# Delta rule layer: softplus, value convolution and key product moved to other slots of the iteration

## The reference

```
q, k, v = silu(causal_conv4(x @ W) + b)              per head
g    = -exp(A_log) * softplus(x @ Wfa @ Wfb + dt_bias)
beta = sigmoid(x @ Wb);  q = l2norm(q) * K**-0.5;  k = l2norm(k)
for each step t:
    S  = S * exp(g)
    vd = (v - S^T k) * beta
    S  = S + k vd^T;  o = S^T q
out = (o * rsqrt(mean(o*o) + eps) * o_norm * sigmoid(gate)) @ Wo
```

## Time and profile before

| | |
|---|---|
| median of 3 runs | 6179.44 us (6178.84 to 6185.34) |
| the profiled execution | 6183.02 us, its span 6181.4 us |
| mean granted clock of PE | 0.925 |
| busy share of the span | PE 80%, PEld 53%, DVE 63%, ACT 44%, POOL 34% |
| the delta rule's 64 iterations | from 1759.6 us on; the last one's Abs (L1875) at 4762.6 us |

### The profile page before, as it was taken

One profiled execution on the slowest core, in us unless ns is written; L12 is line 12 of the kernel. 1 busy time (PEld: TensorE's weight loads), 2 busy tenths in 40 slices (PEclk: granted clock), 3 DMA queues, 4 the chain that ended last, 5 costly groups with the idle time before them and its releaser, 6 DMA issues. The chain is left out here.

```text
span 6181.4 us, 82487 instructions
## 1 busy us (share of the span) xinstructions
PE 4972.5 (80%) x24879; PEld 3272.6 (53%) x24965; DVE 3916.5 (63%) x6588; ACT 2733.2 (44%) x4960; POOL 2091.4 (34%) x2663
## 2 busy tenths in 40 slices
PE   5788747999577888888888888888888665888856
PEld 3566534555245666666666666666666432444423
DVE  4677663222347777777777777777777344888756
ACT  5555351111124444544444444544454212777732
POOL 2455400110234544445444454454544144000100
PEclk8899878999779999999999999999999887999989
DMA  2011005344321111111111111111111034111110
GB/s 59 28 28 29 21 21 193 102 141 154 124 64 55 37 42 37 48 54 44 42 41 48 50 46 40 47 42 41 45 46 30 13 129 136 55 54 53 44 56 27
DMA packets 355561, 365.98 MB, mean 59 GB/s; under 512 B 100192, under 2 KB 253280, under 8 KB 353920
## 3 DMA queue, kind: packets, MB, share of 16 engines
q1 hardware_dynamic: 335472, 286.73, 15.7%
q0 software_dynamic: 19744, 74.99, 3.5%
HBM read 264.76 MB, written 96.86 MB: 59 GB/s over the span
## 5 line engine op out<-in xcount | busy, mean ns | idle before, releaser
L1811 POOL TENSOR_TENSOR delta_rule_suffix<-delta_rule_suffix,delta_rule_prefix 128x256 f32<-128x256 f32 x448 | 499.0, 1114 | 1192.4 <-ACT delta_rule_prefix L1905 767.6
L2152 PE MATMUL delta_rule_proj<-delta_rule_hT,delta_rule_w_qkv 128*128 128x512 f32 x1024 | 468.1, 600 | 0.0
L2176 PE MATMUL delta_rule_level<-delta_rule_qk_second,delta_rule_k_first 128*128 128x128 f32 x3072 | 426.0, 283 | 51.5 <-DVE delta_rule_L_small L1984 40.1
L2176 PEld LDWEIGHTS delta_rule_level<-delta_rule_qk_second,delta_rule_k_first 128*128 128x128 f32 x3072 | 386.1, 195 | 100.0 <-issue 77.9
L481 DVE TENSOR_TENSOR_SCAN scan_hs<-scan_decay,scan_inp 128x512 f32<-128x512 f32 x256 | 308.5, 1216 | 196.2 <-PE scan_inp L543 90.5
L315 POOL TENSOR_TENSOR scan_hc<-scan_hs,scan_c_rows 128x512 f32<-128x512 f32 x256 | 334.5, 1312 | 283.8 <-DVE scan_hs L481 267.8
L1802 POOL TENSOR_TENSOR delta_rule_k_first<-delta_rule_qk,delta_rule_suffix 128x256 f32<-128x256 f32 x384 | 304.7, 793 | 321.4 <-PE delta_rule_level L2164 289.7
L2053 DVE TENSOR_TENSOR delta_rule_prefix<-delta_rule_prefix 128x256 f32<-128x256 f32 x448 | 286.8, 640 | 134.0 <-PE delta_rule_level L2164 95.0
L1995 DVE TENSOR_TENSOR delta_rule_qk_second<-delta_rule_qk,delta_rule_prefix 128x512 f32<-128x512 f32 x448 | 339.6, 758 | 47.5 <-issue 12.1
L1939 ACT ACTIVATE delta_rule_R<-delta_rule_inv 128x512 f32<-128x512 f32 x192 | 114.7, 597 | 571.1 <-PE delta_rule_inv L2211 571.1
L2000 DVE SCALAR_TENSOR_TENSOR delta_rule_qk<-delta_rule_proj,delta_rule_conv_w,delta_rule_qk 128x511 f32<-128x511 f32 (+2 forms) x384 | 287.3, 748 | 109.2 <-ACT delta_rule_qk L1882 82.3
(11 more groups left out here) (465 smaller groups left out, 11612.9 us busy)
## 6 DMA issues: line engine op xcount, KB each, us to landing
parts_dram<-qkv_parts POOLq DMA_DIRECT2D x64, 512.0 KB, 10.5
moe_w_d<-in_w_down SPq DMA_DIRECT2D x39, 512.0 KB, 4.3
scan_c_rows<-bc_dram SPq DMA_DIRECT2D x64, 256.0 KB, 3.5
delta_rule_w_qkv<-in_kda_wq SPq DMA_DIRECT2D x64, 256.0 KB
delta_rule_w_qkv<-in_kda_wk SPq DMA_DIRECT2D x64, 256.0 KB
delta_rule_w_qkv<-in_kda_wv SPq DMA_DIRECT2D x64, 256.0 KB
delta_rule_inv_beta<-beta_dram SPq DMA_DIRECT2D x64, 256.0 KB
delta_rule_w_o<-in_kda_wo SPq DMA_DIRECT2D x64, 256.0 KB, 4.9
```

Of the source, the lines that this page charges most:

```text
L1811: pool.tensor_tensor(first, first, whole_second, ALU.mult).then_inc(suffix_done, 1)
L2152: last = pe.matmul(to, w_qkv[p][:, i, k, :], hT[:, b % 2, k, :], start=(k == 0), stop=(k == DT - 1))
L2176: last = pe.matmul(level_ps[(i + 1) % 2][:, c, :], left, qk_second[:, i % 2, :, c * CHUNK // 2:(c + 1) * CHUNK // 2], start=True, stop=True)
```

## The change

Slots of four things are moved; no operation is added to or taken from the source. ACT does Ln of `u1` in slot 1 (it was in slot 5), and DVE the three softplus operations in slot 4 (slot 6). The first tap of v on ACT goes from slot 6 to slot 4, the other three on DVE from slots 8, 8, 9 to 6, 6, 7. The key product on DVE goes from slot 7 to slot 8, where it stands behind the last `rhs` subtraction.

```diff
@@ -1613,11 +1613,11 @@
         GATE_SLOT, NORM_K_SLOT = 4, 5
         SOLVE_SLOT = 5
         CONV_SLOTS, SILU_SLOTS = (1, 2), (1, 3)
-        V_PROJ_SLOT, V_OUT_SLOT, CONV_V_SLOTS = 3, 6, (8, 8, 9)
+        V_PROJ_SLOT, V_OUT_SLOT, CONV_V_SLOTS = 3, 4, (6, 6, 7)
         SILU_V_SLOT, V_SLOT = 3, 7
         SQUARE_SLOT, NORM_SLOT, LN_SLOT, EXP_SLOT, GATED_SLOT, OUT_SLOT, ADD_SLOT = 12, 13, 20, 20, 26, 23, 26
         VD_COPY_SLOTS = (1, 4, 6, 10)
-        RHS_SLOTS, STATE_SLOTS, KEY_SLOT = (0, 3, 6, 8), (2, 5, 7), 7
+        RHS_SLOTS, STATE_SLOTS, KEY_SLOT, SOFTPLUS_SLOT = (0, 3, 6, 8), (2, 5, 7), 8, 4
 
         DECAY, Q, KEY, K_NORM = range(4)
         PROJ = 4
@@ -1876,6 +1876,9 @@
                         act.activation(z[:], flat(proj_ps[0]), ACT.Identity, bias=dt_bias[:, h:h + 1]).then_inc(bank_read[0], 1)
                         act.wait_ge(abs_done, n + 1)
                         act.activation(e[:], e[:], ACT.Exp, scale=-1.0).then_inc(exp_done, 1)
+                    if slot == 1:
+                        act.wait_ge(u1_done, n + 1)
+                        act.activation(lnu[:], u1[:], ACT.Ln).then_inc(ln_done, 1)
                     if slot in (0, 1):
                         act.wait_ge(proj_done, PROJ * n + Q + slot + 1)
                         reach(act, state_ops_done, n - 1)
@@ -1893,8 +1896,6 @@
                             reach(act, k_turned, n)
                             act.activation(k_square[:], qk[p][:, 1, :], ACT.Square).then_inc(squared, 1)
                     elif slot == NORM_K_SLOT:
-                        act.wait_ge(u1_done, n + 1)
-                        act.activation(lnu[:], u1[:], ACT.Ln).then_inc(ln_done, 1)
                         act.wait_ge(norm_scaled, n + 1)
                         act.activation(k_scale[:], k_scale[:], ACT.Ln).then_inc(norm_ln, 1)
                     elif slot == 6:
@@ -2025,7 +2026,7 @@
                                                  ALU.add, ALU.mult).then_inc(norm_scaled, 1)
                         dve.wait_ge(norm_scaled, n + 1)
                         dve.engine_nop().then_inc(bank_read[0], 1)
-                    elif slot == 6:
+                    elif slot == SOFTPLUS_SLOT:
                         dve.wait_ge(ln_done, n + 1)
                         dve.scalar_tensor_tensor(lnu[:], u1[:], 1.0, lnu[:], ALU.is_gt, ALU.mult)
                         dve.drain()
```

## The result

The changed kernel takes 6074.91 us (median of 4 runs, 6072.74 to 6078.08) against 6182.39 us for the kernel before (4 runs, 6178.84 to 6191.02). The ratio is 0.9825, 95% interval 0.9808 to 0.9842, which is 1.75% faster. The profiled execution took 6075.61 us, its span is 6074.0 us.

The account below looks back on a forecast made before the run. It took PE's own work plus its waits up to the first level product, with a half-clock stretch each iteration, as the bound. 60 iterations at 1.7 us give 102 us, so 6179.4 - 102 = 6077 us; range 6020 to 6130 us.

Parts of the forecast that it names:

- Ln in slot 1 is covered: ACT before the first k tap: the added table load and Ln end 0.8 us before the tap can start; price 0.
- The rival of the dearer table load: ACT slot 1: the load costs 1.9 us or more, the k tap comes 0.6 us late; 6150 us, chance 0.05.
- Softplus in slot 4 costs nothing: DVE before chunk 1's state addition: softplus ends 0.7 us before DVE is needed, even with one operation doubled; price 0.
- The state addition 0.41 us earlier, `vd` of chunk 3 0.67 us earlier: DVE in chunk 2 and ACT in chunk 3: state addition 0.41 us and `vd` copy 0.67 us earlier.
- PE works without a real gap except in the second half of the sequential part: PE in a delta rule iteration: idle only there, 0.85, 0.59 and 1.07 us, then 0.38 us before the first level product.
- First level product 21.12 us in, no longer waiting: PE in the delta rule: L2164 starts 21.12 us into the iteration instead of 22.33, saving 1.2 us at equal clock.
- Free iteration 45.2 us, low one 46.9 us: Changed iteration lengths: 45.2 us without a low PE clock stretch, 46.9 us with one wholly in dense work.
- Low stretches in part of the iterations, so the middle: PE half-clock stretches fall in some iterations only; middle length 46.05 us, 1.74 us less than now.
- 60 iterations at 1.7 us: Whole run: 60 of the 64 iterations each save 1.7 us, 102 us in total.
- the settling: Iterations settle at 47.79 us against low clock stretches at fixed moments; after the change even the longest, 46.9 us, is shorter.
- the low stretches begin at moments that do not depend on the iteration: PE clock: low stretches come at fixed moments, about 3.4 us long, and after the change slide against the iteration.

Follow-up runs that it names:

- The last run: Changed kernel with five unread matrix products in PE's idle places and the four `v_rows` copies on ACT moved from slot 7 to slot 11: 6005.23 us.
- the filled kernel before: Kernel before the change, with five unread matrix products added in PE's idle places of the last two chunks: 6117.85 us, ratio 0.9892.
- the delay that costs nothing: Kernel before the change, with two unread fp32 products, some 0.45 us of PE time, added in slot 13: 6184.54 us, ratio 1.0003.
- the same delay that costs 45 us after the change: Changed kernel with two unread fp32 products, some 0.45 us of PE time, added in slot 13: 6119.93 us, ratio 0.9896 to the kernel before.
- the key product's move that gives 10 us for 0.41 us of path: Changed kernel with the key product put back from slot 8 to slot 7: 6170.88 us, ratio 0.9974 to the kernel before.
- the filling: Five unread matrix products in PE's idle places of the last two chunks: 6117.85 us on the kernel before, 6028.71 us on the changed kernel.

## Why the prediction was right

Forecast 6077 us, measured 6074.91 us. Step by step:

- *Ln in slot 1 is covered.* Right. Load and Ln end 0.77 us ahead of the k tap (0.8 us worked out), and load and Ln are 1.30 us apart. The rival of the dearer table load is out: by the Trainium skill ("ScalarE: Activation LUTs", What ACT_TABLE_LOAD costs) the tap would have come 0.6 us late, and it came at 7.19 us as before.
- *Softplus in slot 4 costs nothing.* Right where the solver doesn't run, where DVE idles 0.89 us behind it. Mis-sized where it does: 3.86 us, for the 2.33 us plus at most one doubled operation that I allowed. The prediction takes softplus to have one operation with two tensor inputs; all three have two (`u1` and `lnu`, `lnu` and `e`, `z` and `lnu`), and all three are slower (0.81, 1.84 and 1.05 us). Of the 0.84 us by which the state addition of chunk 1 is late, the other waits take most; at full clock L2165 comes 0.24 us later, and these iterations last 45.43 or 47.06 us for 45.19 or 46.82 us.
- *The state addition 0.41 us earlier, `vd` of chunk 3 0.67 us earlier.* Right: 17.57 us in for 17.98 (4119.35 in the first iteration), and 20.00 us in (4121.78) for 20.67. The last run confirms that the `v_rows` copies are what held `vd`.
- *PE works without a real gap except in the second half of the sequential part.* Not right as it stands. PE also waits 0.95 us for `rhs` in chunk 1 (L2233), 0.54 us at L2176, 41 us in, and 1.01 us here in the kernel before:

```profile
...
2544.22 1.13 PE L2211 MATMUL delta_rule_inv<-delta_rule_RT,delta_rule_R 128*128 128x128 f32 x8 [1.01 <-DVE delta_rule_X L2087]
...
```

  In the changed kernel these waits are 0.95, 0.54 and 0.99 us in the first iteration. The change leaves them as they were, so the sum did not suffer from it.
- *First level product 21.12 us in, no longer waiting.* Right: 21.11 us without the solver, no wait.
- *Free iteration 45.2 us, low one 46.9 us.* Right: 45.19, and 46.82 to 47.07 us. The free iteration before, which the prediction had at 46.4 us, is 46.49 us in the filled kernel before.
- *Low stretches in part of the iterations, so the middle.* Right in kind: 27 of the last 56, often every other one. That the share came out near one half is luck in part: the prediction took the middle and worked out no share, and with 0.45 us more in each iteration the share is 40 of 56.
- *60 iterations at 1.7 us.* The 56 iterations from iteration 7 on last 46.23 us on average where they lasted 47.93, so 1.69 us less and 95 us together. Another 14 us come from the first seven iterations (the first Abs stands 1.2 us later, which leaves 107), 9 of them from the first three, which have no back part and so no `rhs` or `vd` to come earlier. The prediction itself names these seven as different and others as drawn out, and 60 does not follow from that; the sum came out close because the first seven saved as much for a reason that it does not give and that stays open.

That the settling is a mechanism and not just a story to fit rests on four runs: the delay that costs nothing (6184.54), the same delay that costs 45 us after the change, the key product's move that gives 10 us for 0.41 us of path, and the filling that frees the clock and gives 63 us before and 46 us after. The path alone, 1.22 us in 60 iterations, would have given 73 us. The change gave 107 us. That the low stretches begin at moments that do not depend on the iteration is the prediction's reading; the runs agree with it, and none of them tests it by itself.

It also shows what was in the change. Neither part that was run alone does it: softplus alone 0, the v taps alone +134 us, both without the key product -10 us, all three -107 us. The key product alone, and the key product with one of the others, were not run. Each part that is missing leaves an operation in front of the state addition or the last `rhs`, and the last 0.8 us of path, which the key product brings, take the iteration out of the place where it had settled.

What stays open: which iterations of the changed kernel get a low stretch, as PE's use ahead of it is alike in both kinds, why 16 iterations of the filled kernel before still had one, and how much of softplus' 3.86 us is due to which of the solver's operations.

## What to carry to other kernels

Look at the period of a loop together with the granted clock. If nearly all iterations have exactly the same length and a short low stretch sits at the same place in each, a saving or a delay on the path may show no effect at first and more than its size later. Judge an edit by the start of the bounding instruction within the iteration, and not by the total alone. Before shaving the path, it can pay to fill PE's idle places with work nobody reads: five small products gave 46 us here without touching the path.

## What the hardware showed that I had not expected

- Iterations settle to 47.79 us within about eight iterations after a disturbance, and with 0.45 us more work in each they settle to the same 47.79 us, the low stretch beginning 20.7 instead of 21.7 us in. They come to it from longer iterations and from shorter ones.
- In the changed kernel free and low iterations alternate for long stretches (45.19, 47.07, 45.20, 47.07 us).
- DVE beside POOL: the softplus operation on two SBUF tiles took 1.84 us beside a 1.77 us operation of POOL, against 0.69 us. The Trainium skill ("GPSIMD Engine Reference", Key points) says that POOL shares its SBUF interfaces with DVE and that instructions with two SBUF inputs contend. The trace agrees: 1.84 against 0.69 us. In the iteration before, without POOL's work, it was 0.69 us.
